# The first attention layer in an order of its own over three batches, with every fourth turned tile copied out by ScalarE

## The reference, cut to what matters

```python
x = x + _L0_gnn_ref(_layernorm(x), adj, ...)   # attention over the graph, 4 heads: the stage changed here
x = x + _L0_ffn_ref(_layernorm(x), ...)        # Mamba-2 block
x = x + _L1_gnn_ref(_layernorm(x), adj, ...)   # attention over the graph, 1 head
x = x + _L1_ffn_ref(_layernorm(x), ...)        # LSTM
```

```python
h = nodes @ W[head]                                   # nodes: the layer-normed x
weight = leaky_relu(e_src[i] + e_dst[j], 0.01)        # e_src, e_dst: one number per node and head
weight = where(adj == 0, -1e9, weight)
attention = softmax(weight, axis=-1)                  # 512 x 512
out = relu(attention @ h + bias) + h
out = layernorm(out) * gamma + beta                   # over the head's 64 columns
```

## Time and profile before

| | us |
|---|---|
| median of 3 runs | 4832.03 (4829.57 to 4834.06) |
| profiled execution, its own time | 4839.06 |
| span of the profiled execution | 4837.3 |
| first attention stage, start to its last `XO` pass | 1248.9 |
| one batch in its steady stretch | 37.03 |

### The profile page before, as it was taken

How to read it: one execution, slowest core, us unless ns; L and a number is a source line. 1 busy time by engine, 2 the same in 40 slices (tenths; PEclk the granted TensorE clock), 3 DMA queues, 4 the chain that set the end, 5 groups by cost and what they waited for, 6 DMA issues and landing times. The chain is left out here.

```text
span 4837.3 us, 142627 instructions
## 1 busy us (share of the span) xinstructions
PE 4119.1 (85%) x55809; PEld 2885.5 (60%) x55809; DVE 3534.2 (73%) x8962; ACT 2911.6 (60%) x7074; POOL 1201.2 (25%) x1028
## 2 busy tenths in 40 slices
PE   7888888888399999999998999975888888888882
PEld 4444444444156666666665788854777777777772
DVE  5888888888388888888887677753666666666666
ACT  5777777777298888888886666641333332333330
POOL 3666666665222222222222000000000000000000
PEclk9999999999699999999999999987999999999996
DMA  2121111111100000000001333331111111111115
GB/s 61 60 63 54 53 62 62 53 53 45 53 23 27 27 27 27 27 23 23 27 27 39 109 119 116 118 108 24 34 40 41 39 37 41 42 34 40 43 30 158
DMA packets 326283, 252.58 MB, mean 52 GB/s; under 512 B 171244, under 2 KB 289772, under 8 KB 323564
## 3 DMA queue, kind: packets, MB, share of 16 engines
q1 hardware_dynamic: 324076, 235.03, 16.8%
q10 hardware_dynamic: 1536, 8.39, 0.6%
HBM read 159.42 MB, written 67.11 MB: 47 GB/s over the span
## 5 line engine op out<-in xcount | busy, mean ns | idle before, releaser
L2309 PE MATMUL lstm_G_psum<-lstm_Whh,lstm_HT 128*32 128x192 f32 x8192 | 440.4, 333 | 268.1 <-DVE lstm_HT L2486 267.8
L847 DVE CUSTOM_DVE_ANT_0 g_S<-g_Z_psum,g_relu 128x512 f32<-128x512 f32 x640 | 438.3, 685 | 301.6 <-ACT g_relu L617 299.7
L617 ACT ACTIVATE g_relu<-g_Z_psum,g_src 128x512 f32<-128x512 f32 x640 | 436.8, 682 | 291.0 <-PE g_Z_psum L463 288.7
L2379 ACT ACTIVATE lstm_TC<-lstm_G_psum 128x192 f32<-128x192 f32 x512 | 170.9, 334 | 708.5 <-PE lstm_G_psum L2309 708.5
L473 PE MATMUL g_PT_psum<-g_ident,g_PR 128*128 128x128 f32 x2560 | 398.9, 279 | 158.3 <-DVE g_PT L855 92.3
L473 PEld LDWEIGHTS g_PT_psum<-g_ident,g_PR 128*128 128x128 f32 x2560 | 301.7, 142 | 354.1 <-ACT g_PR L651 237.2
L1785 ACT ACTIVATE ssm_EX<-ssm_Z_psum,ssm_tok 128x256 f32<-128x256 f32 (+1 forms) x1024 | 372.6, 424 | 155.1 <-PE ssm_Z_psum L1615 85.5
L651 ACT ACTIVATE g_PR<-g_S,g_nmax 128x512 f32<-128x512 f32 x640 | 456.9, 714 | 0.1
L2301 PE MATMUL lstm_G_psum<-lstm_Wih,lstm_XT 128*32 128x192 f32 x8192 | 428.0, 327 | 0.0
L2309 PEld LDWEIGHTS lstm_G_psum<-lstm_Whh,lstm_HT 128*32 128x32 f32 x8192 | 214.2, 109 | 355.2 <-DVE lstm_HT L2486 321.5
L2475 DVE SCALAR_TENSOR_TENSOR lstm_AB<-lstm_TC 128x128 f32<-128x128 f32 x512 | 150.2, 293 | 335.5 <-ACT lstm_TC L2379 331.5
(11 more groups left out here) (266 smaller groups left out, 10614.2 us busy)
## 6 DMA issues: line engine op xcount, KB each, us to landing
g_ADJ<-in_adj SPq DMA_DIRECT2D x64, 1024.0 KB, 5.6
x<-g_XO SPq DMA_DIRECT2D x64, 512.0 KB, 3.4
g_X<-in_x SPq DMA_DIRECT2D x32, 512.0 KB, 4.3
ssm_X<-x SPq DMA_DIRECT2D x32, 512.0 KB, 3.9
x<-ssm_OUT SPq DMA_DIRECT2D x32, 512.0 KB, 2.9
g_X<-x SPq DMA_DIRECT2D x32, 512.0 KB, 3.9
lstm_raw<-x SPq DMA_DIRECT2D x1024, 16.0 KB, 1.8
lstm_U<-x SPq DMA_DIRECT2D x128, 128.0 KB, 3.5
```

What stands on the lines that cost most here:

```text
L617: act.activation(relu[n % 4][:, :], score_bank(b, n)[:, :], ACT.Relu, scale=(1.0 - ALPHA) / ALPHA, bias=src[b.slot][:, t, HH * p + hh:HH * ...
L847: v.tensor_tensor_reduce(S[n % 4][:, :], score_bank(b, n)[:, :], relu[n % 4][:, :], -1.0, 3e38, ALU.add, ALU.min, nmax[:, n % 4:n % 4 + 1] ...
L2309: ins = pe.matmul(bank[32 * j:32 * (j + 1), 0:last - first], HT[t % 2][:, 32 * kc:32 * (kc + 1)], Whh[:, kc, j, first:last], start=False, ...
```

## The change

`build` calls a new function `first_attention_phase` for layer 0. The instructions of an item and of the steps around it are the same, with the same shapes, apart from the copy of the turned tiles: items 3, 7, 11 and 15 are copied out by ScalarE (`ACT.Copy`), the other twelve by VectorE as before. Each engine's queue is now a list, `period(b)`, written out operation by operation and repeated for every batch; the lists of one k reach over batches k - 2 to k + 1 on ACT and DVE, k - 1 to k + 1 on PE. Where a step used a bank fixed by its code, a table (`BANK`, `BEFORE`, `DRAIN`) says which of A0 and A1 it takes and whose drain it waits for. The three score banks, two PT banks, four tiles each of `relu`, `S` and `PR`, the one ADJ buffer and three X buffers remain. relu 0 now waits for the first stage of `split`, not for the last. In the set-up, norm_stats of batch 0 comes after the constants.

```diff
+def first_attention_phase(nc, nb, x_in, adj, weights, consts, x_out, kept):
...
+        Zb = [m.ps(f"Z{k}") for k in range(3)]
+        PTb = [m.ps(f"PT{k}") for k in range(2)]
+        Ob = m.ps("O")
+        Ab = [m.ps(f"A{k}") for k in range(2)]
...
+        DRAIN = {"xnt0": (("xt", 2, 1),), "xnt1": (("xt", 2, 2),), "pj0": (("h", 2, 1),), "pj2": (("h", 2, 2),),
+                 "co0": (("s1", 1, 1),), "pt": (("rows", 1, 1),), "ob0": (("d1", 2, 1),), "ob1": (("d1", 2, 2),)}
+        BANK = {"xnt0": Ab[1], "xnt1": Ab[0], "pj0": Ab[0], "pj2": Ab[1], "co0": Ab[1], "pt": Ab[1], "ob0": Ab[0],
+                "ob1": Ab[0]}
+        BEFORE = {"xnt0": (("pj2", -1),), "xnt1": (("pj0", -1), ("ob1", -2),), "pj0": (("xnt1", 0),), "pj2": (("pt",
+                  0),), "co0": (("xnt0", 0),), "pt": (("co0", 0),), "ob0": (("pj0", 1), ("ob1", -1),), "ob1": (("ob0",
+        def bank_free(b, op):
+
+            for was, ago in BEFORE[op]:
+                if 0 <= (b + ago).off < nb:
+                    for sem, per, count in DRAIN[was]:
+                        (b + ago).wait(nc.tensor, s[sem], per, count)
...
+        def evacuated(eng, b, n):
+
+            shared = (n + 1) // EVERY
+            b.wait(eng, s["ev"], ITEMS - ITEMS // EVERY, n + 1 - shared)
+            b.wait(eng, s["ev_a"], ITEMS // EVERY, shared)
...
+            def load_x(b):
+                if b.off == 0:
+                    return
+                b.wait(sp, s["xb"], 1, 1 - SLOTS)
+                b.wait(sp, s["xn"], IT, (1 - SLOTS) * IT)
+                sp.dma_start(X[b.slot][:, :, :], xv[b.index()]).then_inc(x_loaded[b.slot], 16)
+
+            def load_adj(b):
+                b.wait(sp, s["mask"], 1, 0)
+                b.wait(sp, s["check"], IT, 0)
+                sp.dma_start(ADJ[:, :, :], av[b.index()]).then_inc(s["adj_loaded"], 16)
+
...
+            def turn(b, n):
+                b.wait(pe, s["p"], ITEMS, n + 1)
+                evacuated(pe, b, n - 2)
+                for k in range(IT):
+                    ins = pe.transpose(PTb[n % 2][:, k * P:(k + 1) * P], PR[n % 4][:, k * P:(k + 1) * P], ident[:, :])
+                ins.then_inc(s["t"], 1)
...
+            def evacuate(b, n):
+                p, t, hh = item(n)
+                b.wait(act, s["t"], ITEMS, n + 1)
+                b.wait(act, s["pv"], NP, p + 1 - NP)
+                act.activation(PT[HH * p + hh][:, :, t * P:(t + 1) * P],
+                               PTb[n % 2][:, :].rearrange("p (k i) -> p k i", k=IT), ACT.Copy).then_inc(s["ev_a"], 1)
...
+        @block.sync
...
+            def period(b):
+                at(b, store)
+                at(b + 4, load_adj)
+                at(b + 4, load_x)
+
+            for k in range(-4, nb + 0):
+                period(Batch(None, k, SLOTS))
...
+        @block.tensor
...
+            def period(b):
+                at(b + -1, turn, 3)
+                at(b + -1, turn, 4)
+                at(b, xn_turned, 1)
+                at(b + -1, scores, 9)
+                at(b + -1, scores, 10)
+                at(b + -1, turn, 5)
+                at(b + -1, scores, 11)
+                at(b, columns, 0)
+                at(b + -1, scores, 12)
+                at(b, columns, 1)
+                at(b + -1, turn, 6)
+                at(b + -1, turn, 7)
+                at(b, project, 0)
+                at(b + -1, turn, 8)
+                at(b, project, 1)
+                at(b + -1, scores, 13)
+                at(b + -1, weigh, 0, 0)
+                at(b + -1, turn, 9)
+                at(b + -1, scores, 14)
+                at(b + -1, weigh, 0, 1)
+                at(b + -1, scores, 15)
+                at(b + -1, turn, 10)
+                at(b, parts_turned)
+                at(b + -1, weigh, 0, 2)
+                at(b + -1, turn, 11)
+                at(b + -1, turn, 12)
+                at(b, scores, 0)
+                at(b + -1, weigh, 0, 3)
+                at(b, scores, 1)
+                at(b + -1, turn, 13)
+                at(b, scores, 2)
+                at(b, project, 2)
+                at(b, scores, 3)
+                at(b + -1, turn, 14)
+                at(b, project, 3)
+                at(b + -1, turn, 15)
+                at(b, scores, 4)
+                at(b + -1, outputs_turned, 0)
+                at(b, turn, 0)
+                at(b + -1, weigh, 1, 0)
+                at(b + -1, weigh, 1, 1)
+                at(b, turn, 1)
+                at(b, scores, 5)
+                at(b, scores, 6)
+                at(b + -1, weigh, 1, 2)
+                at(b + -1, weigh, 1, 3)
+                at(b, scores, 7)
+                at(b, turn, 2)
+                at(b, scores, 8)
+                at(b + -1, outputs_turned, 1)
+                at(b + 1, xn_turned, 0)
+
+            for k in range(-1, nb + 1):
+                period(Batch(None, k, SLOTS))
...
+        @block.scalar
...
+            def period(b):
+                at(b + -1, h_out, 0)
+                at(b + -2, exp, 14)
+                at(b + -1, relu_part, 1)
+                at(b + -2, exp, 15)
+                at(b + -2, o_out, 0)
+                at(b + -1, exp, 0)
+                at(b + -1, relu_part, 2)
+                at(b + -2, evacuate, 15)
+                at(b + -1, relu_part, 3)
+                at(b + -1, exp, 1)
+                at(b + -1, relu_part, 4)
+                at(b + -1, exp, 2)
+                at(b + -1, exp, 3)
+                at(b + -1, relu_part, 5)
+                at(b + -1, h_out, 1)
+                at(b + -1, relu_part, 6)
+                at(b + -1, exp, 4)
+                at(b + -2, o_out, 1)
+                at(b + -1, relu_part, 7)
+                at(b + -1, relu_part, 8)
+                at(b + -1, exp, 5)
+                at(b + -1, evacuate, 3)
+                at(b, xt_out, 0)
+                at(b, xt_out, 1)
+                at(b + -1, relu_part, 9)
+                at(b + -1, relu_part, 10)
+                at(b + -1, exp, 6)
+                at(b + -1, relu_part, 11)
+                at(b + -1, exp, 7)
+                at(b + -1, relu_part, 12)
+                at(b + -1, exp, 8)
+                at(b + -1, exp, 9)
+                at(b + -1, evacuate, 7)
+                at(b + -2, square)
+                at(b + -1, exp, 10)
+                at(b + -1, exp, 11)
+                at(b + -1, relu_part, 13)
+                at(b + 1, check, 0)
+                at(b + 1, check, 1)
+                at(b + 1, check, 2)
+                at(b + -1, exp, 12)
+                at(b, rows_out)
+                at(b + -1, relu_part, 14)
+                at(b + -1, relu_part, 15)
+                at(b + 1, check, 3)
+                at(b + -1, exp, 13)
+                at(b + -1, evacuate, 11)
+                at(b, relu_part, 0)
+
+            for k in range(-1, nb + 2):
+                period(Batch(None, k, SLOTS))
...
+        @block.vector
...
+            def period(b):
+                at(b, split, 0)
+                at(b + -1, evacuate, 8)
+                at(b, split, 1)
+                at(b + -1, evacuate, 9)
+                at(b, split, 2)
+                at(b + -1, leaky, 13)
+                at(b + -1, evacuate, 10)
+                at(b + 1, norm_stats)
+                at(b + -1, leaky, 14)
+                at(b + -1, evacuate, 12)
+                at(b + -1, leaky, 15)
+                at(b, leaky, 0)
+                at(b + -1, evacuate, 13)
+                at(b, leaky, 1)
+                at(b + -1, evacuate, 14)
+                at(b + -1, recip)
+                at(b + 1, make_mask, 0)
+                at(b, leaky, 2)
+                at(b + 1, make_mask, 1)
+                at(b, leaky, 3)
+                at(b + 1, make_mask, 2)
+                at(b + 1, make_mask, 3)
+                at(b, evacuate, 0)
+                at(b, leaky, 4)
+                at(b + -1, normalise, 0)
+                at(b, evacuate, 1)
+                at(b, leaky, 5)
+                at(b, leaky, 6)
+                at(b, evacuate, 2)
+                at(b, leaky, 7)
+                at(b + -1, normalise, 1)
+                at(b, leaky, 8)
+                at(b, evacuate, 4)
+                at(b + -1, residual)
+                at(b, leaky, 9)
+                at(b + -1, residual_sum)
+                at(b, evacuate, 5)
+                at(b, evacuate, 6)
+                at(b, leaky, 10)
+                at(b, leaky, 11)
+                at(b, leaky, 12)
+                at(b + -1, squares_sum)
+
+            for k in range(-1, nb + 1):
+                period(Batch(None, k, SLOTS))
...
+        @block.gpsimd
...
+            def period(b):
+                at(b + 1, bias_added)
+                at(b, centred)
+                at(b, residual)
+                at(b, layernorm, 0)
+                at(b, layernorm, 1)
+                at(b, layernorm, 2)
+                at(b, layernorm, 3)
+                at(b + 3, normalised)
+
+            for k in range(-3, nb + 0):
```

(3 more changed lines are left out.)

355 lines of the change are left out of this document (added).

## The result

| | before | after |
|---|---|---|
| median of 4 runs each | 4830.8 us (4827.99 to 4834.06) | 4614.97 us (4613.57 to 4618.85) |
| profiled execution, its own time | 4839.06 us | 4613.81 us |
| end of the stage's last `XO` pass | 1248.9 us | 1028.2 us |
| one batch in the steady stretch | 37.03 us | 30.26 us |

The ratio is 0.9554, with 95% [0.9538, 0.9571]: 216 us less, where 177 was forecast. In the profiled executions the stage ends 220.7 us earlier and the rest of the program takes 3583.8 instead of 3588.4 us, 4.6 us that are within what two runs differ by.

The account below looks back on a forecast made before the run. No engine was full, so the order bounded the stage. New ring (3), 26.8 + M of 4.6, plus 0.2 gave 31.6 us a batch; 30 x 5.4 = 163 plus 13.5 of ramps, 177 off 4832: 4655 us, range 4618 to 4735.

Parts of the forecast that it names:

- The bound of before: Old stage, 37.03 us a batch: no engine full; the order bounds it, through a ring of waits across PE, ACT and DVE.
- The engines' lists: Each engine's queue without waits, per batch: PE floor 30.5 us, ACT 29.6 start to start, DVE 25.0 without masks.
- M: Time of the four masks in DVE's list, beside POOL's normalised passes: taken as 4.6 us, bounds 1.4 to 8.0.
- ring (3): Longest ring: ACT's queue from relu 8 to next relu 1, DVE's leaky 1 to 5, scores 8: 26.8 + M, 31.4 us.
- only the engines' floors count: Rival: masks fall in POOL's gaps, ring (3) is 28.2 and PE's 30.5 us binds: 4623 us; chance 15%.
- 0.2 for what two nearly full engines lose to each other: Allowance per batch added to ring (3)'s 31.4 us, giving 31.6 us.
- Ramps: Stage's start and end: 9 us less up to batch 1, 4.5 less at the tail, 13.5 together.
- Copies hold up ACT: Rival: ScalarE's four copies each wait 1 us, ring (3) takes two: 33.6 us a batch, 4716 us; chance 8%.
- The ring of SP: Rival: DVE's norm_stats waits for load_x, which waits for XB; landing 11 us after XB gives 4844 us; chance 4%.
- The rule of the shared ports: VectorE and GpSimd: whichever starts first holds the port pair for its whole instruction; a mask beside HB took 1.41 against 0.41 us.

Follow-up runs that it names:

- copies_only: Kernel before, its order kept, with only items 3, 7, 11 and 15 of a batch copied out by ScalarE: 4835.33 us, ratio 1.0008.
- old_masks_late: Kernel before, its four masks moved from steps 4, 5, 6 and 8 to steps 11 to 14, beside normalised's passes: 4829.09 us, ratio 0.9988.
- order_only_b: Kernel after, all sixteen copies on VectorE, with the copy of item 7 placed before leaky 12: 4629.59 us, ratio 0.9575.
- two_more: Kernel after, each check writing its own tile, and norm_stats and normalised of batch 0 ahead of the constants' set-up: 4601.16 us, ratio 0.9517.
- xn_two_inputs: Kernel after, POOL's four one-input passes of normalised replaced by two two-input passes of 128x1024: 4660.70 us, ratio 0.9644.
- masks_early: Kernel after, the four masks moved up VectorE's list to where POOL runs the layer norm's two-input passes: 4685.41 us, ratio 0.9695.
- both_less: Kernel after, without the checks of tiles 1 to 3 and without the second head of each weigh but the first: 4600.31 us, ratio 0.9514.

## Why the prediction was right, and where it failed

- **The bound of before: right.** No engine was full, and taking time off one brought nothing: 2.4 us off DVE 0.0 (copies_only), 1.9 us off DVE 0.23 (old_masks_late). Where the order was changed and the copies were not, 93% of the gain was there (order_only_b).
- **The engines' lists: right within 0.8 us.** PE was put at 30.5 with 0.3 for a lower clock; alone it fills 29.72, at a granted clock of 1.00 throughout. ACT was put at 29.6; it fills 29.86, by the checks' waits for each other (two_more took them away, 0.29 us a period). DVE without masks was put at 25.0; measured are 26.4 - 1.8 = 24.6 as busy time.
- **M in ring (3): the step that failed.** "Beside XN (...) I take 0.9 + 1.1 + 1.0 + 1.6 = 4.6": it measured 1.6, near its lower bound of 1.4. I had carried the delay seen beside HB over to passes of another kind, which the trace of before never showed beside a mask. With 1.6 the ring is 28.4 and not the longest; what then binds are PE and ACT, as in the rival "only the engines' floors count" (4623, 15%), though for another reason than its gaps: masks ran inside passes in 0.42 us, and one was held up by 0.2. (31.6 - 30.26) x 30 = 40 us are nearly all of the 44 us by which the traces' gain, 220.7, exceeds the 177 forecast; the rest is the ramps.
- **Ring (3) without M: 1.0 us too short.** It binds when M is large (xn_two_inputs), but DVE's wait for relu 2 (0.7) and the checks' waits (0.28) are not in it. With them the kernel after has 26.8 + 1.6 + 1.0 = 29.4, still under PE and ACT, so this cost the forecast nothing. Had M been 4.6, the forecast would have been 1 us a batch too low; that 31.82 came with M = 3.95 is two errors that nearly cancel.
- **0.2 for what two nearly full engines lose to each other** was small: 0.4 to 0.5, of which the trace shows 0.36 as PE's one wait for ACT's copy.
- **Ramps:** scores 0 of batch 1 at 66.0 (predicted 67), the tail 54.9 (57): 16.9 us instead of 13.5. Scores 0 of batch 0 came at about 40.7 (its second matmul at 40.96, less 0.22), not 38.
- **Copies hold up ACT: wrong, as thought.** PE waits for a copy 0.36 us once a batch, and ACT's copies wait for nothing. The ring of SP didn't appear either: no wait of a statistic for a load.
- **The rule of the shared ports, that the later instruction waits out the earlier: only in part.** The masks of xn_two_inputs and masks_early end 0.28 us after the pass they met; so does the last mask of the kernel after, but the mask before it takes 0.42 us inside the same pass, and those of order_only_b end 0.26 us or more before theirs. Of the port pair that VectorE and GpSimd share the Trainium skill, "SBUF — State Buffer", section "SBUF: two separate sides", says the later one "fully blocks". Beside the two-input passes of 128x1024 the traces agree; beside normalised they mostly don't, and the measurement decides.

Open: what it is in POOL's pass that holds a mask up. The passes that did were all tensor_tensor with two inputs and 128x1024 elements; those of normalised are tensor_scalar with one input and 128x256. Number of inputs, operation and size changed together, in xn_two_inputs too, so the first theory is not shown against the other two. One row speaks against inputs or operation alone: the small two-input tensor_tensor of 128x4 (615.63, 1.04 us) didn't hold up the mask inside it (0.36). Open too is what binds at 28.5.

## What to carry to other kernels

When no engine is full, price the cyclic order, not the instructions: an edit worth 2 us of an engine brought nothing, and one copy three places off cost 77 us. Before a term decides which ring binds, ask whether any row shows that very pair of operations side by side; if none does, forecast both rings and their floors, not the middle. An edit that is to free an engine must be seen to free it in the trace before its time is read.

## What was not expected of the hardware

- A mask (int32 to bfloat16, 128x512) on VectorE takes 0.42 to 0.68 us beside GpSimd's one-input passes of 128x256, and up to 1.97 beside two-input ones of 128x1024, ending 0.28 us after them.
- Four of those one-input passes take 4.86 us alone (two_more, at the start) and 5.44 in the kernel after. The masks aren't what makes them longer as a rule: with no mask beside them they take 5.51 in the kernel before, and with four, 5.05 in order_only_b. In old_masks_late they take 6.10. Which of VectorE's instructions lengthens them wasn't separated.
- The matmuls of 64 columns for two heads run side by side: 1.07 us for one head's pair of records, 1.08 for two heads' four (both_less).
- A wait of ScalarE for its own preceding instruction costs 0.14 us (0.86 and 0.84 from start to start instead of 0.71).
